# Column sums of the projection weights by two-column products, one row broadcast through DRAM, and half an embedding in between

## The reference

```
pe   = conv(pixels, conv_w, stride 14)                 # 6 x 6 patches of 256 channels: 4 windows of 9
red  = mean of pe over the 9 patches of a window
q    = ln(red, q_g, q_b) @ la_wq                        # ln: (x - mean) * rsqrt(var + 1e-5) * g + b
kv   = ln(win, kv_g, kv_b) @ la_wkv
agg  = softmax(q k / 16) v        over the 9 patches, 8 heads of 32
local_out = red + agg @ la_proj_w + la_proj_b
gq   = ln(class_emb, gq_g, gq_b) @ ga_wq
gkv  = ln(local_out, gkv_g, gkv_b) @ ga_wkv             # attention of the class token over 4 windows
out  = concat(local_out @ mod_w + mod_b, class token)
```

## Time and profile before

| what | value |
|---|---|
| median of three runs | 558.89 us |
| the profiled execution | 557.25 us, span 555.5 us |
| TensorE matmul busy | 472.1 us (85%) |
| VectorE busy | 397.1 us (71%) |
| ScalarE busy | 231.3 us (42%) |
| GpSimd busy | 225.5 us (41%) |
| granted TensorE clock over the span | 0.926 |

### The profile page before, as it was taken

How to read it: one execution, slowest core, us unless ns; L and a number is a source line. 1 busy time by engine, 2 the same in 40 slices (tenths; PEclk the granted TensorE clock), 3 DMA queues, 4 the chain that set the end, 5 groups by cost and what they waited for, 6 DMA issues and landing times. The chain is left out here.

```text
span 555.5 us, 6685 instructions
## 1 busy us (share of the span) xinstructions
PE 472.1 (85%) x1748; PEld 232.2 (42%) x1748; DVE 397.1 (71%) x738; ACT 231.3 (42%) x420; POOL 225.5 (41%) x199
## 2 busy tenths in 40 slices
PE   6989999999999899999518658878787778889997
PEld 3634655655655665446415311212121212266653
DVE  0066666666666684557989648999999998768664
ACT  1112112122113114789576435767676767312100
POOL 5000100100100212024976417999999999742000
PEclk9999999999999999997659866999998987999999
DMA  9970029000000004000563774676766666410000
GB/s 271 312 238 27 1 81 299 26 1 0 2 0 0 1 1 131 12 0 1 159 170 98 210 194 108 174 190 153 180 188 174 164 168 180 128 49 1 19 9 19
DMA packets 37947, 57.47 MB, mean 103 GB/s; under 512 B 5781, under 2 KB 28753, under 8 KB 37923
## 3 DMA queue, kind: packets, MB, share of 16 engines
q1 hardware_dynamic: 37266, 56.45, 36.5%
q10 hardware_dynamic: 656, 0.73, 0.4%
HBM read 38.19 MB, written 18.84 MB: 103 GB/s over the span
## 5 line engine op out<-in xcount | busy, mean ns | idle before, releaser
L1614 POOL TENSOR_TENSOR gb<-da,hb 128x512 f32<-128x512 f32 x96 | 120.6, 1280 | 16.3 <-ACT da L1554 14.5
L1554 ACT ACTIVATE da<-da 128x512 f32<-128x512 f32 x128 | 78.7, 629 | 50.1 <-DVE da L1642 47.7
L1642 DVE TENSOR_TENSOR da<-ps,expA 128x512 f32<-128x512 f32 x128 | 84.1, 687 | 3.9 <-PE ps L1470 3.6
L302 PE MATMUL ps<-xbuf,convw 128*128 128x384 f32 (+1 forms) x240 | 81.9, 494 | 5.5 <-DMA convw<-in_conv_wT 5.5
L1470 PE MATMUL ps<-drows,selb 96*128 96x512 bf16 x128 | 52.7, 425 | 32.1 <-DVE da L1642 25.7
L356 PE MATMUL ps<-wall,peT 128*128 128x512 f32 x144 | 67.7, 593 | 0.0
L302 PEld LDWEIGHTS ps<-xbuf,convw 128*128 128x128 f32 (+1 forms) x240 | 45.7, 193 | 36.8 <-ACTq L499 4.1
L1659 DVE TENSOR_TENSOR hb<-gb,ps 128x512 f32<-128x512 f32 x80 | 54.0, 682 | 0.9 <-POOL gb L1614 0.4
L1470 PEld LDWEIGHTS ps<-drows,selb 96*128 96x128 bf16 x128 | 12.9, 101 | 97.6 <-DVE da L1642 86.2
L1480 PE MATMUL ps<-urows,brows 96*128 96x512 bf16 x128 | 44.0, 433 | 3.7 <-DVE gb L1649 3.1
L526 ACT ACTIVATE kvs<-ps 128x512 f32<-128x512 f32 x36 | 21.5, 598 | 57.4 <-PE ps L356 57.4
(11 more groups left out here) (220 smaller groups left out, 790.6 us busy)
## 6 DMA issues: line engine op xcount, KB each, us to landing
xbuf<-in_xT SPq DMA_DIRECT2D x11, 768.0 KB
yscr<-yst SPq DMA_DIRECT2D x30, 208.0 KB
dparts<-dpt SPq DMA_DIRECT2D x30, 128.0 KB, 2.4
uparts<-upt SPq DMA_DIRECT2D x30, 128.0 KB, 2.4
drows<-dparts SPq DMA_DIRECT2D x16, 240.0 KB, 3.0
urows<-uparts SPq DMA_DIRECT2D x16, 240.0 KB, 3.9
brows<-bparts SPq DMA_DIRECT2D x16, 240.0 KB, 4.4
urows<-uparts SPq DMA_DIRECT2D x16, 160.0 KB, 4.1
```

Source lines behind the costliest of these rows:

```text
L302: mm = pe.matmul(bank(T_EMB + j % 2, 0, EN), convw[0:n, k, h * P:(h + 1) * P], xbuf[0:n, q, k, c * EN:(c + 1) * EN], start=(k == 0), stop= ...
L1554: act.activation(da[:, j, :], da[:, j, :], ACT.Exp, scale=-1.0).then_inc(da_ready, 1)
L1614: pool.tensor_tensor(gb[:, j, :], da[:, j, :], hb[:, d, (s_ - 1) % 2, :], ALU.mult).then_inc(gp_done, 1)
L1642: dve.tensor_tensor(da[:, j, :], bank(j % 2), expA[:, j % 2, :], ALU.mult).then_inc(e_free, 1)
```

## The change

The offset row and the column sum of the gained weights are the same kind of product: one with the column `b`, one with the column `g`, both on the weights as they were loaded. `column_sums(i)` computes both at once, with a left operand of two columns (`gain_offset`, a view of the vector tile), into two partitions of PSUM. ScalarE copies the 2 x 1536 results to `vrow` (a view of `gkvs`, not yet in use), SP stores them to a scratch row pair `scr` in DRAM and reads each row back to 128 partitions: the sums to `mrow` (a view of `kvs`, second buffer), the offsets to `brow`. `centre(i)` now subtracts 1/256 of the sum, by one scalar_tensor_tensor from SBUF. All four sums and gains run ahead of the tokens; columns 0 to 2 of `embedding(1)` stand between the sums and `tokens(0)`, columns 3 to 5 behind it. On VectorE the centring of gkv and gq is ahead of `attention_end(0)`. The exponential of window 0 is ahead of column 5 on ScalarE. On SP there is a new wait for the last tile of the first product ahead of all further loads, and the round trip stands ahead of `rows` and the projections.

The diff, without lines that only declare semaphores and tiles:

```diff
...
 LB = [[7] * 5, [7] * 5, [7] * 5, [1, 2, 3, 4, 6]]
-PREP = [("q", 6, 2), ("kv", 7, 3), ("gkv", 7, 7), ("gq", 7, 7)]
+PREP = [("q", 6, 0), ("kv", 7, 0), ("gq", 6, C), ("gkv", 4, 0)]
+vrow = gkvs[0:2, :, :].rearrange("p w n -> p (w n)")[:, 0:1536]
+mrow = kvs[:, 1, 0:3, :].rearrange("p k n -> p (k n)")
+gain_offset = cols[:, 0:16].rearrange("p (s j h) -> p s j h", j=2, h=CH)
+VS = {"q": 0, "gq": 1, "kv": 2, "gkv": 3}
 PARTS3 = [(0, 3), (3, 6), (6, 9)]
 def halves(n):
...
                 load_x_tile(sp, k)
             else:
                 load_conv_tile(sp, k)
+        sp.wait_ge(k_landed[KC - 1], 32)
         load_x(0, 1)
         load_x(0, 2)
         sp.dma_start(cols[:, :], a["vec_cols"]).then_inc(s_vec, 16)
...
         sp.dma_start(wall[:, :, :], a["wall"].rearrange("(h p) n -> p h n", p=P)).then_inc(s_wall, 16)
         for c in range(EC):
             load_x(1, c)
-
+        sp.wait_ge(s_rows, 3)
+        sp.dma_start(scr, vrow).then_inc(s_rows, 16)
+        sp.wait_ge(s_rows, 19)
+        sp.dma_start(mrow, scr[0:1, :].to_broadcast([P, 1536])).then_inc(s_mrow, 16)
+        sp.dma_start(brow[:, :], scr[1:2, :].to_broadcast([P, 1536])).then_inc(s_brow, 16)
         sp.dma_start(rows[:, :], a["vec_rows"].to_broadcast([P, NVR])).then_inc(s_proj, 16)
         for n, name in enumerate(["la_proj_w", "ga_proj_w", "mod_w"]):
             sp.dma_start(projw[:, n], a[name].rearrange("(h p) n -> p h n", p=P)).then_inc(s_proj, 16)
...
     @block.tensor
     def _(pe):
-        def embedding(w, between=()):
+        def embedding(w, between=(), js=range(CH * EC)):
             q = w % 2
             for c in range(EC):
                 for h in range(CH):
                     j = c * CH + h
+                    if j not in js:
+                        continue
                     if j < len(between) and between[j]:
                         between[j]()
                     if h == 0 and (w, c) != (0, 0):
...
                                        start=(k == 0), stop=(k == KC - 1))
                     mm.then_inc(emb_ready, 1)
-        def offset(i):
-            s, b_, _ = PREP[i]
+        def column_sums(i):
+            s, b_, at = PREP[i]
             o, n = SEG[s]
             if i == 0:
                 pe.wait_ge(s_vec, 32)
                 pe.wait_ge(s_wall, 16)
-            if i >= 2:
-                pe.wait_ge(s_brow, i)
-                pe.wait_ge(s_wready, 4)
             for h in range(CH):
-                mm = pe.matmul(bank(b_, 0, n), col(s + "_b", h).to_broadcast([P, P]), wall[:, h, o:o + n],
+                mm = pe.matmul(ps[0:2, b_ * 512 + at:b_ * 512 + at + n], gain_offset[:, VS[s], :, h], wall[:, h, o:o + n],
                                start=(h == 0), stop=(h == CH - 1))
-            mm.then_inc(s_bias, 1)
-
-        def mean(i):
-            s, _, b_ = PREP[i]
-            o, n = SEG[s]
-            pe.wait_ge(s_wg, 2 * i + 2)
-            if i == 2:
-                pe.wait_ge(s_brow, 4)
-            if i == 3:
-                pe.wait_ge(s_wready, 6)
-            for h in range(CH):
-                mm = pe.matmul(bank(b_, 0, n), onesc[:, :], wall[:, h, o:o + n],
-                               start=(h == 0), stop=(h == CH - 1))
-            mm.then_inc(s_wmean, 1)
+            mm.then_inc(s_sums, 1)
         def turn(w, u, src):
             pe.wait_ge(tr_free, 10 * w + u + 1)
...
             pe.wait_ge(agg_ready, w + 1)
             if w == 0:
                 pe.wait_ge(s_wready, 8)
+                pe.wait_ge(s_brow, 16)
             elif w < W4 - 1:
                 pe.wait_ge(mod_copied, w)
             b_ = LB[w][0]
...
                     lambda: keys_values(w), lambda: out_token(w)]
         embedding(0)
-        for i in range(2):
-            offset(i)
-        for i in range(2):
-            mean(i)
-        pe.wait_ge(s_brow, 2)
+        for i in range(4):
+            column_sums(i)
+        embedding(1, js=range(0, 3))
+        pe.wait_ge(s_rows, 19)
         pe.wait_ge(s_wready, 4)
         pe.wait_ge(s_const, 4)
         tokens(0)
-        embedding(1, [lambda: offset(2), None, lambda: offset(3), None, lambda: mean(2), lambda: mean(3)])
+        embedding(1, js=range(3, 6))
         tokens(1)
         embedding(2, local_steps(0))
         tokens(2)
...
         act.sem_inc(kv_free, 2)
         act.sem_inc(red_kept, 2)
-        def copy_offset(i):
-            s, b_, _ = PREP[i]
-            o, n = SEG[s]
-            act.wait_ge(s_bias, i + 1)
-            act.activation(brow[:, o:o + n], bank(b_, 0, n), ACT.Copy).then_inc(s_brow, 1)
-
-        def embedded(w, between=()):
+        def copy_sums(b_, o):
+            act.activation(vrow[:, o:o + 512], ps[0:2, b_ * 512:(b_ + 1) * 512], ACT.Copy).then_inc(s_rows, 1)
+
+        def embedded(w, between=(), js=range(CH * EC)):
             q = w % 2
             for c in range(EC):
                 for h in range(CH):
                     j = c * CH + h
+                    if j not in js:
+                        continue
                     for f in (between[j] if j < len(between) else ()):
                         f()
                     act.wait_ge(emb_ready, 6 * w + j + 1)
...
             act.activation(gkvs[:, w, :], bank(LB[w][3]), ACT.Copy).then_inc(gkv_copied, 1)
         embedded(0)
-        copy_offset(0)
-        copy_offset(1)
+        act.wait_ge(s_sums, 4)
+        copy_sums(6, 0)
+        copy_sums(7, 512)
+        copy_sums(4, 1024)
+        embedded(1, js=range(0, 3))
         keys_values(0)
-        embedded(1, [[lambda: copy_offset(2)], [], [lambda: exponential(0), lambda: copy_offset(3)]])
+        embedded(1, [[], [], [], [], [], [lambda: exponential(0)]], js=range(3, 6))
+        act.wait_ge(s_wready, 8)
         keys_values(1)
         for w in (2, 3):
             embedded(w, [[lambda: agg_copied(w - 2)], [], [lambda: exponential(w - 1)], [lambda: lo_copied(w - 2)],
...
     @block.vector
     def _(dve):
         ch = Chain(dve, d_chain)
-        dve.memset(onesc[:, :], 1.0 / C)
         dve.sem_inc(tr_free, 2)
         dve.sem_inc(kvs_free, 2)
         dve.sem_inc(q_free, 1)
...
         def gain(i):
             s = PREP[i][0]
             o, n = SEG[s]
-            dve.wait_ge(s_bias, i + 1)
+            dve.wait_ge(s_sums, i + 1)
             for h in range(CH):
                 dve.tensor_scalar(wall[:, h, o:o + n], wall[:, h, o:o + n], col(s + "_g", h), None,
                                   ALU.mult).then_inc(s_wg, 1)
         def centre(i):
-            s, _, b_ = PREP[i]
+            s = PREP[i][0]
             o, n = SEG[s]
             dve.wait_ge(s_wg, 2 * i + 2)
-            dve.wait_ge(s_wmean, i + 1)
+            dve.wait_ge(s_mrow, 16)
             for h in range(CH):
-                dve.tensor_tensor(wall[:, h, o:o + n], wall[:, h, o:o + n], bank(b_, 0, n),
-                                  ALU.subtract).then_inc(s_wready, 1)
+                dve.scalar_tensor_tensor(out=wall[:, h, o:o + n], in0=mrow[:, o:o + n], scalar=-1.0 / C,
+                                         in1=wall[:, h, o:o + n], op0=ALU.mult, op1=ALU.add).then_inc(s_wready, 1)
         def window_mean(w):
             q = w % 2
...
         def query(w):
             dve.wait_ge(rstd_ready, 2 * w + 1)
             dve.wait_ge(q_ready, w + 1)
-            dve.wait_ge(s_brow, 2)
+            dve.wait_ge(s_brow, 16)
             dve.scalar_tensor_tensor(out=qn[:, :], in0=bank(T_Q, 0, C), scalar=rstd[:, K9:K9 + 1],
                                      in1=brow[:, 0:C], op0=ALU.mult, op1=ALU.add).then_inc(q_free, 1)
             dve.wait_ge(q_free, w + 2)
...
                                   ALU.mult).then_inc(xn_ready, 1)
         dve.wait_ge(s_vec, 32)
-        gain(0)
-        gain(1)
+        for i in range(4):
+            gain(i)
         centre(0)
         centre(1)
         dve.wait_ge(s_wready, 4)
         attention_begin(0)
         softmax(0)
-        gain(2)
-        gain(3)
-        attention_end(0)
         centre(2)
         centre(3)
+        attention_end(0)
         for w in (1, 2):
             attention_begin(w)
             softmax(w)
...
         dve.wait_ge(gq_read, 1)
         dve.wait_ge(grs_ready, 1)
-        dve.wait_ge(s_brow, 4)
+        dve.wait_ge(s_brow, 16)
         ch.link(dve.scalar_tensor_tensor(out=gqn[:, :], in0=gqraw[:, :], scalar=grs[:, W4:W4 + 1],
                                          in1=brow[:, C:2 * C], op0=ALU.mult, op1=ALU.add))
```

More of the change, by code:

```diff
@@ L114, in tower @@
         bparts = nc.dram_tensor("bparts", (NG, 12, GB, 2 * L * P), BF16, kind="Internal").ap()
+        scr = nc.dram_tensor("scr", (2, 1536), F32, kind="Internal").ap()
         NY = 3 * 32 + GB
@@ L135, in tower @@
         convw = sb("convw", [P, KC, C], ctx=tok)
-        onesc = sb("onesc", [P, P], ctx=tok)
         xbuf = sb("xbuf", [P, 2, KC, WT], ctx=tok)
@@ L170, in tower @@
         s_const, s_dtz = sem("s_const"), sem("s_dtz")
-        s_bias, s_brow = sem("s_bias"), sem("s_brow")
```

(3 more changed lines are left out.)

## The result

The changed kernel takes 566.12 us (median of four, 565.09 to 568.81), beside 559.4 for the kernel before on the same chip: a ratio of 1.012, with a 95% interval of 1.0079 to 1.016. It is slower by 1.2%. The forecast was 560.4, with a range of 555.0 to 565.5: the time lies outside it. The profiled execution took 565.09 us, span 563.3, against 557.25 and 555.5.

A forecast was written before the change was run, and what follows sets the result against it. TensorE was taken to bound the token phase as long as VectorE keeps up. Terms -5.15 - 2.05 - 2.5 + 1.4 + 7.25 + 2.6 = +1.55 us gave 560.4 us on the median's scale, range 555 to 565.5.

The forecast's parts named there:

- the fence: At the start, SP holds other loads until the first product's last tile pair lands; claimed -2.5 us, bounds 0 and -3.1.
- the fence gives nothing: Rival at the start: chunk 1 or the weights eat the gain; +4.05 us, 562.9; chance 0.13.
- The rows of this kernel's start don't show that: Said of the skill page's low default clock: granted clock is 1.00 over the first 26.6 us despite 4.16 us without work.
- Products, -5.15: In the weight preparation ahead of the tokens, eight products become four, so TensorE loses four: -5.15 us.
- waits, -2.05: TensorE's waiting within the 7.20 us of weight preparation ahead of the first tokens goes away: -2.05 us.
- The round trip, +1.4: Ahead of the first tokens, sums go through DRAM and back under three embedding columns; TensorE waits +1.4 us, bounds 0 and 5.
- The late broadcast: Rival ahead of the first tokens: means take 7 us instead of 4.2, and the clock falls; +6.95 us, 565.8; chance 0.15.
- VectorE's tail, +7.25: In window 1's tokens TensorE stops after two and waits for VectorE's work behind the first tokens: +7.25 us, bounds 6.3 and 8.5.
- The clock, +2.6: Behind the long wait in window 1's tokens the granted clock falls to the 1.2 GHz level: +2.6 us, bounds 0 and 3.0.
- The rival that it holds: Rival in window 1's tokens: the clock does not fall behind the wait, as at the start; -1.05 us, 557.8; chance 0.20.
- the rearrangement: Forecast terms other than the fence, up to the end of window 1's tokens: products, waits, round trip, VectorE's tail, clock; +4.05 us.

The follow-up runs named there:

- 64 + 12 rows: The changed kernel, fence included, with every 76-row tile loaded as 64 rows and 12 rows: median 560.98 us, ratio 1.001 to the kernel before.
- the kept-busy run: The changed kernel plus eight unused products between second and third token of window 1, where TensorE waits for VectorE: ratio 1.001 to the kernel before.
- the fastest kernel: The changed kernel without fence, with split 76-row loads, two columns ahead and four behind, later global centring, earlier exponential, sums copied singly: 556.22 us, ratio 0.9949.

## Why the prediction was wrong

**The step that failed is the fence: "Kept apart they land at about 7.0", "I take -2.5; bounds 0 ... and -3.1".** It cost 3.22 in the profiled execution, a miss of 5.7, as large as the distance from 560.4 to 566.1; what else was off, -1.5 and +2.0, nearly cancels, by luck. Three sizes make up the 5.7:

- I spread 1.51 MB over all queues, while the last tile pair goes over 4 of 16 engines: the fence opened at 8.9 instead of 7.1, 1.8 us (shown by the tail in the trace, and by its absence with 64 + 12 rows).
- I gave chunk 1 4.3 us from issue to use, from a load at 78.4 us; it took 6.4, 2.1 more, with its own 76-row part on the same four engines and chunk 2 and the weights issued right behind it. From 9.00 to 15.35 the queues moved 6.35 x 243 = 1.54 MB, of which chunk 1 is 0.90: the loads behind it moved beside it. (5.4 with the rows split; the rest isn't separated.)
- I counted no clock behind a wait of this length, "no fall behind 1.39 at the start": behind 2.29 it fell, for 1.8 us.

The bound of 0 left no room for a loss, and the rival I had for it, "the fence gives nothing", ended at 562.9 for the same reason.

**The gain itself was also out of reach, by the clock at the start.** The prediction has the first eight matmuls at 0.32 us each and reads the granted clock of 1.00 as full speed from the launch on. Both are wrong. The first row below is from the first matmul on, the second is as long and lies behind the wait for the last tile (kernel before, columns as in rows 1; a matmul that reaches into a window is counted):

```profile
...
4.16:7.49 3.33, 3.33 (x5) 1.80 (x6) 0.00 (x0) 0.60 (x1) 2.78 (x8) 1.00 1.05 324
10.46:13.79 3.33, 3.33 (x12) 2.00 (x11) 0.00 (x0) 0.49 (x1) 0.00 (x0) 1.00 1.08 313
...
```

Five matmuls against eleven and the end of one: from 4.93 to 7.49 they start 0.64 us apart, behind that 0.32. The record of the granted clock has its first entry, 1.00, at 7.51; the 1.00 that the windows show ahead of it stands for no entry. All 14 traces are alike in this, with first entries from 7.0 to 10.5. So the sentence "The rows of this kernel's start don't show that" was a misreading: TensorE starts at the low level here, behind 4 us without work. In the changed kernel the eighth matmul starts at 8.60 and the ninth at 8.93, with no wait for the last tile in between, so two columns end, and chunk 1 is wanted, at 13.06 instead of 10.9. Had it been there in time, the start would have been about 13.06 + 4 x 3.23 = 26.0 by my estimate: a gain of 0.9, not 2.5.

**Products, -5.15, and waits, -2.05:** right. Four two-column products take 35.39 - 30.14 = 5.25 us; two columns instead of 128 bought nothing.

**The round trip, +1.4:** 0.1. Copies 1.54 instead of 1.8, store 1.5 from 37.06 instead of 2.1, means 4.4 instead of 4.2, centring 1.97 instead of 2.5; the first tokens start 15.04 us behind the sums, when the three columns have just ended. The late broadcast didn't come.

**VectorE's tail, +7.25:** 6.97, from 78.32 to 85.29. It resumes 7.33 us behind the end of the first tokens (forecast 7.55), the aggregate ends at 15.67 (15.9), TensorE restarts at 20.53 (20.9).

**The clock, +2.6:** 102.52 - 85.29 = 17.23 instead of 14.70: 2.53, and 2.49 by the kept-busy run. In the other four runs of the same wait it was 1.5 to 2.5, so that it came this near to 2.6 is in part luck. The rival that it holds falls: behind a wait of 6.8 it fell all five times, and what spoke for it, the start's rows, was the misreading above.

So the rearrangement was forecast at +4.05 and came at +2.54; the start was forecast at -2.5 and came at +3.22; the stretch behind 250 us added 1.9, which I had put at nothing. Together +7.8 on the profiled spans. The change was forecast as no difference, with 0.17 for slower by over 1%; it is slower by 1.2%, by a mechanism that no rival named.

## What to carry to other kernels

A fence that gives the first transfers the queues for themselves costs what the slowest of them takes on the engines that it really uses, and gives only what TensorE could have used earlier; look at the DMA share just before the fence opens, and at the row counts of the tiles. Take TensorE's speed at the start from the distance of the matmuls' starts, not from the clock column. Work laid under a wait is taken from where it stood: ask what it hid there (here VectorE's tail of 20.5 us, with TensorE through in 13.6). Two waits of 2 us cost less here than one of 7, since the long one also brought the low clock with it.

## What the runs showed of the hardware

In all 14 traces the matmuls of the first product start 0.64 us apart at first and 0.32 us apart from 7.0 to 10.5 us on, where the record of the granted clock begins; where no tile is waited for, a later rise is a later start (10.52 against 8.47: 1.01 us). A 76-row transfer runs on a quarter of the engines: 0.25 of the share and 90 GB/s, against 280 GB/s and more at full share; 64 and 12 rows don't show this. The granted clock fell behind waits of TensorE of 6.8 us in all five traces that have one, of 5.22, and of 3.6 in both; of 3.17, 2.64, 2.50 and 2.29 in one trace each, and not behind 3.06 and 2.30 in others; 2.00 and 2.19 in the fastest kernel left it at 1.00, but 2.18 in the first product without the fence did not. Between 2.2 and 3.2 us the length alone doesn't decide. One row of 6 KB in DRAM, read by 128 partitions, landed in 4.4 us (768 KB), and the second one, issued right behind it, in 5.9; plain loads issued into idle queues had moved 0.78 MB in 4.0 us.
